# First cross attention: the second temper matmul goes behind the next scores, and the norm's mix and the next group's values change places in the slots

## The chip, the cores and the metric

The kernel runs on one core of a Trainium2 chip (trn2). A core has five engines that run their own instruction queues and meet only through semaphores: PE (TensorE, matmuls and transposes into PSUM), DVE (VectorE), ACT (ScalarE, activation functions), POOL (GpSimd) and SP (here only the issuer of DMAs). The metric is the device time of one execution in microseconds (us), the median over runs.

## The reference

A decoder of two layers works on `x` of 32 sequences x 128 tokens x 128 features and a context of 32 x 77 x 128, all in float32. Each layer is self attention (in the first layer a gated recurrence), cross attention to the context and a feed-forward part, each with a residual and a layer norm. The change is in the first layer's cross attention, which has 16 heads of 8 features:

```python
qk = jnp.einsum('bhqd,bhkd->bhqk', Q, K)
scores = qk / math.sqrt(dk)
mean_sim = scores.mean(axis=(-2, -1))
max_sim = scores.max(axis=-1).mean(axis=-1)
probs = jax.nn.softmax(scores, axis=-1)
entropy_proxy = jnp.var(probs, axis=-1, ddof=1).mean(axis=-1)
feats = jnp.stack([mean_sim, max_sim, entropy_proxy], axis=-1)
hidden = jax.nn.gelu(_linear(feats, w1, b1), approximate=False)
hidden = jax.nn.gelu(_linear(hidden, w2, b2), approximate=False)
log_t = jnp.clip(_linear(hidden, w3, b3), LOG_T_MIN, LOG_T_MAX)
t = jnp.exp(log_t)[..., None]
attn = jax.nn.softmax(qk / (2.0 * t), axis=-1)
out = jnp.einsum('bhqk,bhkd->bhqd', attn, V)
```

So each head of each sequence gets a temperature of its own, from three features of its scores through a small network of three linear steps with two Gelus between them; the real softmax is taken with it. `out` then goes through `Wo`, is added to `x` and normalised.

## The kernel before

`x` stays on chip, transposed, as `xT` (128 features x 4096 tokens). The stages run one after another, each in blocks of its own with its own semaphores. `cross_attention` (line 753) is called twice; only the call with `temper` (the small network's weights) is touched, since the other takes the other list of places.

The 32 sequences stand in 8 groups of 4 (`GB`, `NG`). Work that is done per group: context transpose, keys, queries and values (matmuls over a whole group), the temper network's three matmuls `t1`, `t2`, `t3`, the output projection with the residual (`mix`) and the variance of the norm (`var`). All of these use one PSUM bank, `misc`, in a fixed order: each matmul step waits on `misc_free` until the step before it has been read out, and each reader waits on `misc_mm`. The table `MISC` numbers them in the order in which they stand in `ORDER`.

Work per sequence: `scores` (PE: 8 instructions; DVE: a maximum over the keys, line 1210, then the distance to it, line 1212, each over 128 x 1232), `kbd` (POOL: expands the keys for the scores of the next sequence), `soft` (ACT: exponential, line 1088; POOL: its square), `sums` (DVE: two reductions of them, for the features), `pre` (POOL: distance times the rate), `exp` (ACT, line 1108), `turn` 0 to 3 (PE transposes of the probabilities, evacuated by ACT with Relu, line 1118), `attend` (PE, line 1030), `logs` and `scale` (ACT and DVE: the normalisation of every second sequence's output, line 1248).

There is a software pipeline over slots: slot n works on the scores of sequence n, but on the `pre` and `exp` of sequence n-7, the `turn` of n-8, `attend` of n-9 and the normalisation of n-10. `ORDER` is one list of steps, written out by hand, and every engine goes through the same list and issues its own part of each step; so the list is the queue order of every engine. In each slot it has two places for group work, one after the first two turns and one at the slot's end, after `attend`. `PLACES` says what stands in them in slots 0 to 3 of a group, with an offset of groups: `("values", 1)` are the values of the group after this one, `("mix", -3)` the mix of three groups ago. An entry stands in the list as the step itself (for PE) and then its `_out` (for the engine that reads it from PSUM).

Before, the four slots hold: slot 0 context | keys; slot 1 queries | t1 and t2; slot 2 t3 | values; slot 3 mix | var. The pair `t12` is expanded to `t1, t2, t1_out, t2_out`, so on PE t2 stands right behind t1 and waits on `g1_ready`, which ACT raises in `t1_out`. On ACT, `t1_out` is a Gelu (line 1091) for which a table load is put ahead of it, and `t2_out` (line 1096) is a second Gelu and then an explicit load of the table with Ln and Exp (line 1099):

```python
elif kind == "t2":
    misc(kind, n)
    pe.wait_ge(g1_ready.sem, n + 1)
...
elif kind == "t2_out":
    misc("t2", n)
    f(g2[:, :], ps_m[:, 0:GB * H], ACT.Gelu, bias=mb2[:, :]).then_inc(g2_ready.sem, 1)
    act.wait_ge(g2_ready.sem, n + 1)
    act.sem_inc(misc_free.sem, 1)
    nc.scalar.preload_act_table_set(LN_EXP)
```

`t3` on PE waits on `g2_ready`; `t3_out` on DVE (lines 1239 and 1242) clips; `rate` on ACT (line 1104) makes the factor with which `pre` multiplies. `values_out` is four additions on DVE (line 1198), `mix_out` one on DVE (line 1253, writes `y`), `square` on ACT in slot 3 (line 1128), `var_out` a Ln and an Exp on ACT, and `divide` on DVE in the next slot 0 (line 1258). The step `mean` at the end of slot 2 sums queries and keys on DVE (lines 1230 and 1231).

Of the kernel before, what the change touches and what calls it, by code (L numbers as in the profile page):

```python
# [32 lines left out]
GB = 4  # L33
# [719 lines left out]
def cross_attention(nc, const, tag, xT, context, wq, bq, wk, bk, wv, bv, wo, bo, turn, temper=None):  # L753


    with ExitStack() as ctx:
# [88 lines left out]


        if temper:
            PLACES = [(("context", 1), ("keys", 1)), (("queries", 1), ("t12", -1)), (("t3", -1), ("values", 1)), (("mix", -3), ("var", -3))]
        else:
            PLACES = [(("context", 1), ("keys", 1)), (("queries", 1), ("values", 1)), (None, None), (("mix", -1), ("var", -1))]  # L850

        def place(n, which, read):
            at_ = PLACES[n % GB][which]
            if at_ is None or not 0 <= n // GB + at_[1] < NG:
                return []
            kinds = ("t1", "t2") if at_[0] == "t12" else (at_[0],)
            return [(kind + "_out" * read, n // GB + at_[1], 0) for kind in kinds]

        ORDER = [("bo", 0, 0), ("bo_out", 0, 0)]
        for kind in ("context", "keys", "queries", "values"):  # L860
# [2 lines left out]
        for n in range(B + LA + 4):  # L863
            g, r = n // GB, n % GB
            ORDER += [("scores", n, 0), ("kbd", n + 1, 0)] + [("pre", n - LE, 0)] * bool(temper)
            ORDER += [("turn", n - LT, 0), ("turn", n - LT, 1), ("logs", n - LA - 1, 0), ("scale", n - LA - 1, 0)]
            ORDER += [("divide", g - (4 if temper else 2), 0)] * (r == 0)
            ORDER += place(n, 0, False) + place(n, 0, True)
            ORDER += [("soft", n, 0), ("sums", n - 1, 0)] * bool(temper) + [("exp", n - LE, 0)] * (not temper)
            ORDER += [("turn", n - LT, 2), ("turn", n - LT, 3)]  # L870
            ORDER += [("square", g - (3 if temper else 1), 0)] * (r == 3)
            ORDER += [("exp", n - LE, 0)] * bool(temper) + [("attend", n - LA, 0)]
            ORDER += place(n, 1, False) + place(n, 1, True)
            if temper:
                ORDER += [("feat", g - 1, 0)] * (r == 0) + [("mean", g, 0), ("rate", g - 1, 0)] * (r == 2)
# [1359 lines left out]
def program(nc, a, out):  # L2235

    def of(prefix, *names):
        return [a[f"{prefix}_{n}"] for n in names]

    with ExitStack() as ctx:  # L2240
        xT = ctx.enter_context(nc.sbuf_tensor("xT", [P, NT], F32))
        const = constants(nc, ctx)
        min_gru(nc, const, xT, a["x"], *of("L0_attn", "Wp", "bp", "g1", "Whg", "bhg", "Wo", "bo", "g2", "gf", "Wf", "bf"))
        cross_attention(nc, const, "x0", xT, a["ctx_1024"], *of("L0_xattn", "Wq", "bq", "Wk", "bk", "Wv", "bv", "Wo", "bo"), turn=True,
                        temper=of("L0_xattn", "w1", "b1", "w2", "b2", "w3", "b3"))
        tile_ffn(nc, const, xT, *of("L0_ffn", "signatures_raw", "knot_values", "temperature", "compress_w1", "compress_b1",
                                    "compress_w2", "compress_b2", "spline_w1", "spline_b1", "spline_w2", "spline_b2",
                                    "directions", "norm_gamma", "norm_beta", "output_scale"))
        self_attention(nc, const, xT, *of("L1_attn", "adaptive_scale", "Wq", "bq", "Wk", "bk", "Wv", "bv", "Wo", "bo", "gamma", "beta"))
        cross_attention(nc, const, "x1", xT, a["ctx_1024"], *of("L1_xattn", "W_Q", "b_Q", "W_K", "b_K", "W_V", "b_V", "W_O", "b_O"), turn=False)  # L2250
        moe_ffn(nc, const, xT, *of("L1_ffn", "w_gate", "w_expert", "b_expert"), out)
# [16 lines left out]
```

## Time and profile before

| what | value |
|---|---|
| median of 3 runs | 2020.5 us (2016.04 to 2021.6) |
| profiled execution | 2020.03 us, span 2018.3 us |
| busy over the whole span | PE 84%, PE weight loads 49%, DVE 62%, ACT 59%, POOL 20% |
| mean granted TensorE clock | 0.911 of full |
| first cross attention with its norm | about 737 to 1036 us of the span |

Times are counted from the start of the span. In a timeline each line gives the start, the time (of the merged group where it ends in xN), the engine, the line of the kernel, the operation, what it writes and reads, and in brackets how long the engine had idled before it and what ended that. PEld is the weight load of PE, which overlaps its matmuls. The granted clock is a share of 2.4 GHz; 0.5 is 1.2 GHz.

### The profile page before, as it was taken

The page shows a single profiled execution, that of the slowest core. Times are in us where ns is not written, and L with a number is a line of the kernel's source. Part 1 is how long each engine was busy: PE and PEld are TensorE (multiplying, and loading weights), DVE is VectorE, ACT ScalarE, POOL GpSimd, SP SyncE. Part 2 cuts the span into 40 slices and gives each one's busy share as a digit, 9 for nine tenths or more (in the row PEclk, how much of TensorE's full clock was granted, in tenths as well). Part 3 has the DMA queues.
Part 4 walks back from the last instruction along what each step waited for, and adds up shares of the span by engine and source line. Part 5 has one row for each costly group of instructions (what it writes and reads, how often), then busy time and mean ns, then how long its engine had stood idle before and what let it go on. Part 6 is the DMA issues. An engine that isn't in the chain of part 4 may idle for free. (4 is left out here: it accounts for less than half of the span.)

```text
span 2018.3 us, 30939 instructions
## 1 busy us (share of the span) xinstructions
PE 1695.7 (84%) x11538; PEld 988.3 (49%) x11538; DVE 1252.9 (62%) x1715; ACT 1200.1 (59%) x2551; POOL 400.2 (20%) x369
## 2 busy tenths in 40 slices
PE   3999999999999636888776938999999998688876
PEld 1444444444443213666663414666666666466655
DVE  0777777777778358887527434566666666466644
ACT  2777777787777415787842434555565564355654
POOL 0111011011111026666600001222222222101100
PEclk9999999999999866898975778999999999699997
DMA  4000000000000000000000010000000000000001
GB/s 120 1 11 1 0 7 5 0 0 0 0 0 0 0 21 7 5 5 2 2 4 0 0 42 1 1 1 1 1 1 1 1 1 1 20 8 8 2 4 47
DMA packets 36812, 16.90 MB, mean 8 GB/s; under 512 B 15334, under 2 KB 35520, under 8 KB 36672
## 3 DMA queue, kind: packets, MB, share of 16 engines
q1 hardware_dynamic: 32512, 9.11, 2.0%
q10 hardware_dynamic: 4160, 5.90, 0.9%
q8 instruction: 91, 1.49, 0.3%
q14 instruction: 49, 0.40, 0.1%
HBM read 12.90 MB, written 2.10 MB: 7 GB/s over the span
## 5 line engine op out<-in xcount | busy, mean ns | idle before, releaser
L1967 POOL TENSOR_TENSOR self_probs<-self_probs,self_rz 128x1024 f32<-128x1024 f32 x64 | 121.4, 1897 | 539.5 <-DVE self_rz L1995 539.5
L525 POOL TENSOR_SCALAR gru_decay<-gru_zgate 128x512 f32<-128x512 f32 x96 | 75.8, 790 | 590.7 <-ACT gru_zgate L478 565.5
L1942 ACT ACTIVATE self_probs<-self_scores,self_neg 128x128 f32<-128x128 f32 x512 | 181.9, 386 | 16.6 <-DVE self_neg L1990 16.6
L389 PE MATMUL gru_gate<-gru_xn,gru_whg 128*128 128x512 f32 x384 | 182.4, 597 | 3.5 <-DVE gru_xn L568 3.5
L393 PE MATMUL gru_hid<-gru_xn,gru_whg 128*128 128x512 f32 x384 | 180.4, 592 | 0.0
L401 PE MATMUL gru_out<-gru_y,gru_wo 128*128 128x512 f32 x384 | 178.1, 599 | 0.7 <-DVE gru_y L596 0.6
L1016 PE MATMUL x_turned<-const_ident,x_probs 128*77 128x128 f32 x1024 | 153.0, 297 | 14.2 <-ACT x_pt L1118 9.9
L1118 ACT ACTIVATE x_pt<-x_turned 77x512 f32<-77x512 f32 x224 | 122.1, 584 | 62.9 <-PE x_turned L1016 62.7
L1016 PEld LDWEIGHTS x_turned<-const_ident,x_probs 128*77 128x77 f32 x1024 | 124.6, 159 | 65.2 <-issue 28.7
L1210 DVE TENSOR_REDUCE x_m<-x_scores 128x16 f32<-128x1232 f32 x64 | 91.8, 1434 | 94.8 <-PE x_scores L1005 94.8
L591 DVE SCALAR_TENSOR_TENSOR gru_ghid<-gru_hid,gru_half_c,gru_sighid 128x512 f32<-128x512 f32 x96 | 71.8, 748 | 113.6 <-ACT gru_sighid L479 113.5
L596 DVE TENSOR_TENSOR_SCAN gru_y<-gru_decay,gru_value 128x516 f32<-128x516 f32 x96 | 118.3, 1232 | 3.3
L389 PEld LDWEIGHTS gru_gate<-gru_xn,gru_whg 128*128 128x128 f32 x384 | 72.7, 191 | 94.9 <-issue 94.3
L401 PEld LDWEIGHTS gru_out<-gru_y,gru_wo 128*128 128x128 f32 x384 | 70.2, 190 | 98.4 <-issue 76.1
L393 PEld LDWEIGHTS gru_hid<-gru_xn,gru_whg 128*128 128x128 f32 x384 | 73.1, 190 | 92.3 <-issue 92.3
L1942 ACT ACTIVATION_READ_ACCUMULATOR self_probs<-self_scores,self_neg 128x1 f32 x512 | 115.9, 226 | 0.0
L478 ACT ACTIVATE gru_zgate<-gru_gate,gru_bhg_c 128x512 f32<-128x512 f32 x96 | 66.0, 687 | 67.0 <-PE gru_hid L393 66.3
L344 PE MATMUL gru_stat<-gru_sq,const_ones 128*128 128x512 f32 x144 | 77.2, 626 | 28.6 <-DVE gru_sq L572 28.6
L1928 ACT ACTIVATE self_qT<-self_bank,self_bq,self_scale 128x512 f32<-128x512 f32 x50 | 39.4, 788 | 96.0 <-PE self_bank L1864 96.0
L458 ACT ACTIVATE gru_sq<-gru_h 128x512 f32<-128x512 f32 (+1 forms) x128 | 76.8, 629 | 32.5 <-DVE gru_h L601 30.2
L1030 PE MATMUL x_out<-x_pt,x_vpad 77*32 77x128 f32 x2048 | 69.5, 276 | 30.1 <-DVE x_oT L1248 17.7
L1212 DVE TENSOR_TENSOR x_dist<-x_scores,x_m 128x1232 f32<-128x1232 f32 x64 | 92.2, 1441 | 2.2
(356 smaller groups left out, 3544.5 us busy)
## 6 DMA issues: line engine op xcount, KB each, us to landing
gru_whg<-in_L_attn_Whg ACTq DMA_DIRECT2D x4, 768.0 KB, 10.0
x_ctx_in<-in_ctx SPq DMA_DIRECT2D x16, 154.0 KB
gru_xin<-in_x SPq DMA_DIRECT2D x8, 256.0 KB, 2.9
out<-moe_y SPq DMA_DIRECT2D x8, 256.0 KB, 2.3
gru_wo<-in_L_attn_Wo ACTq DMA_DIRECT2D x4, 384.0 KB, 10.9
self_w_raw<-in_L_attn_Wq SPq DMA_DIRECT2D x1, 512.0 KB, 6.1
self_w_raw<-in_L_attn_Wk ACTq DMA_DIRECT2D x1, 512.0 KB, 6.8
self_w_raw<-in_L_attn_Wv SPq DMA_DIRECT2D x1, 512.0 KB, 9.2
```

The source lines that it names most:

```text
L344: mm(ps_stat[u][:, :], const["ones"][:, :], sq[u][:, 0, :], start=True, stop=True).then_inc(done.sem, 1)
L389: mm(ps_gate[n % 2][:, :], whg[:, l, k, DI + c * P:DI + (c + 1) * P], xn[u][:, k, :], start=(k == 0), stop=(k == KH - 1))
L393: last = mm(ps_hid[n % 2][:, :], whg[:, l, k, c * P:(c + 1) * P], xn[u][:, k, :], start=(k == 0), stop=(k == KH - 1))
L401: last = mm(ps_out[m][:, :], wo[:, l, c, m * P:(m + 1) * P], padded(y[u][:, c, :]), start=(c == 0), stop=(c == KI - 1))
L458: f(sq[u][:, m, :], hidden_chunk(u, i, m), ACT.Square).then_inc(sq_ready[u].sem, 1)
L596: v.tensor_tensor_scan(y[u][:, c, :], decay[r][:, :], value[r][:, :], 0.0, ALU.mult, ALU.add).then_inc(scan_ready.sem, 1)
L1016: last = turn_(ps_t[c % 2][0:S, j * T:(j + 1) * T], probs[n % 2][:, TILE4 * j + c, :], ident[:, :])
L1118: f(pt[n % 2][:, c, :, :].rearrange("p j t -> p (j t)"), ps_t[c % 2][0:S, :], ACT.Relu).then_inc(pt_ready[c].sem, 1)
L1210: v.tensor_reduce(top, scored(), AX.X, ALU.max).then_inc(m_ready.sem, 1)
L1212: v.tensor_tensor(dist[:, n % RING, :, :].rearrange("p (r i) s -> p r i s", i=TILE4), scored(), top.unsqueeze(3).broadcast_to([P, TILE4, T ...
L1942: last = f(probs[n % 2][:, a, jj, :], ps_s[n % 2][:, a, jj * T:(jj + 1) * T], ACT.Exp, bias=neg[n % 2][:, a, jj:jj + 1], accum_out=z[n % 2 ...
L1967: pool.tensor_tensor(probs[n % 2][:, :, :, :], probs[n % 2][:, :, :, :], whole, ALU.mult).then_inc(pn_ready.sem, 1)
```

## The change

The list of places is rewritten and the expansion of an entry changes. After it the four slots hold: slot 0 context | keys; slot 1 queries | t1; slot 2 t2 and t3 | mix; slot 3 values | var. The entry `t23` is expanded to `t2, t2_out, t3, t3_out`, all in its place, so on PE t3 follows t2 directly, and on ACT the second Gelu stands behind the evacuations of turns 0 and 1 of slot 2. `t1_out` stands at the end of slot 1 as before. The offsets in groups stay. No instruction of the kernel's own is added, removed or resized.

```diff
         if temper:
-            PLACES = [(("context", 1), ("keys", 1)), (("queries", 1), ("t12", -1)), (("t3", -1), ("values", 1)), (("mix", -3), ("var", -3))]
+            PLACES = [(("context", 1), ("keys", 1)), (("queries", 1), ("t1", -1)), (("t23", -1), ("mix", -3)), (("values", 1), ("var", -3))]
         else:
...
             at_ = PLACES[n % GB][which]
             if at_ is None or not 0 <= n // GB + at_[1] < NG:
                 return []
-            kinds = ("t1", "t2") if at_[0] == "t12" else (at_[0],)
-            return [(kind + "_out" * read, n // GB + at_[1], 0) for kind in kinds]
+
+            if at_[0] == "t23":
+                return [] if read else [(kind, n // GB + at_[1], 0) for kind in ("t2", "t2_out", "t3", "t3_out")]
+            return [(at_[0] + "_out" * read, n // GB + at_[1], 0)]
```

## Rows read from the trace of the kernel before

**Rows 1.** Windows: busy us of each engine, clock, DMA; steady part of the stage.
```profile
780.00:960.00 180.00, 146.94 (x1942) 110.82 (x1945) 146.53 (x158) 133.05 (x199) 120.29 (x94) 0.86 0.01 4
```

**Rows 2.** Waits of the whole stage: us in total, times, longest us.
```profile
DVE x_m L1210 <- PE x_scores L1005: 37.8, 15, 4.4
...
PE x_misc L1042 <- ACTq L1093: 16.2, 8, 2.8
```

**Rows 3.** Timeline, group 4: end of slot 1 and begin of slot 2.
```profile
868.11 0.39 PE L1037 MATMUL x_misc<-x_var_f,x_w1b 128*128 128x64 f32 x2
868.72 1.28 ACT L1091 ACT_TABLE_LOAD   x1
...
870.02 0.31 ACT L1091 ACTIVATE x_g<-x_misc,x_mb 128x64 f32<-128x64 f32 x1
...
870.48 0.41 PE L1042 MATMUL x_misc<-x_g,x_w2T 128*128 128x64 f32 x2 [1.98 <-ACTq L1093]
...
870.81 0.80 PE L1005 MATMUL x_scores<-x_kbd,x_q 32*128 32x308 f32 x8
870.92 0.32 ACT L1096 ACTIVATE x_g<-x_misc,x_mb 128x64 f32<-128x64 f32 x1 [0.59 <-PE x_misc L1042]
...
871.75 1.44 DVE L1210 TENSOR_REDUCE x_m<-x_scores 128x16 f32<-128x1232 f32 x1 [3.44 <-PE x_scores L1005]
...
872.48 0.33 PE L1046 MATMUL x_misc<-x_g,x_w3b 128*128 128x64 f32 x2
872.63 1.08 ACT L1118 ACTIVATE x_pt<-x_turned 77x512 f32<-77x512 f32 x2
```

**Rows 4.** Timeline, group 4: rest of slot 2 and begin of slot 3.
```profile
873.28 1.15 PE L1016 MATMUL x_turned<-const_ident,x_probs 128*77 128x128 f32 x8 [0.46 <-ACT x_pt L1118]
...
874.77 1.23 ACT L1088 ACTIVATE x_e<-x_dist 128x1232 f32<-128x1232 f32 x1 [1.06 <-DVE x_dist L1212]
...
876.24 1.10 PE L995 MATMUL x_misc<-x_w_v,x_cT 128*77 128x128 f32 x8
...
877.80 0.87 DVE L1198 TENSOR_TENSOR x_vpad<-x_misc,x_bv_row 77x128 f32<-77x128 f32 x4
...
879.07 1.02 PE L1050 MATMUL x_misc<-x_oT,x_w_o 128*128 128x512 f32 x2
...
879.57 1.43 DVE L1210 TENSOR_REDUCE x_m<-x_scores 128x16 f32<-128x1232 f32 x1
```

**Rows 5.** Group 5: its scores and first values in slot 2, and a window there.
```profile
902.47 0.80 PE L1005 MATMUL x_scores<-x_kbd,x_q 32*128 32x308 f32 x8
...
908.82 1.10 PE L995 MATMUL x_misc<-x_w_v,x_cT 128*77 128x128 f32 x8
...
904.00:908.00 4.00, 4.00 (x56) 3.84 (x58) 3.82 (x5) 3.04 (x5) 0.21 (x1) 0.66 0.00 0
```

**Rows 6.** Timeline, group 4: slot 3, `mix_out`, and attention behind DVE's normalisation.
```profile
882.72 0.74 DVE L1253 SCALAR_TENSOR_TENSOR x_y<-x_misc,x_b_o,xT 128x512 f32<-128x512 f32 x1
882.86 1.08 PE L1030 MATMUL x_out<-x_pt,x_vpad 77*32 77x128 f32 x32 [1.89 <-DVE x_oT L1248]
```

**Rows 7.** Timeline, groups 1 and 2: the maximum in slot 2.
```profile
776.51 1.44 DVE L1210 TENSOR_REDUCE x_m<-x_scores 128x16 f32<-128x1232 f32 x1 [2.48 <-PE x_scores L1005]
...
805.84 1.44 DVE L1210 TENSOR_REDUCE x_m<-x_scores 128x16 f32<-128x1232 f32 x1 [4.37 <-PE x_scores L1005]
```

**Rows 8.** Timeline, group 8: the last t2, after the last scores.
```profile
997.40 0.41 PE L1042 MATMUL x_misc<-x_g,x_w2T 128*128 128x64 f32 x2 [1.25 <-ACTq L1093]
```

**Rows 9.** Timeline: the maximum in slot 0 of groups 5 and 6.
```profile
887.39 1.44 DVE L1210 TENSOR_REDUCE x_m<-x_scores 128x16 f32<-128x1232 f32 x1 [1.00 <-PE x_scores L1005]
...
921.40 1.44 DVE L1210 TENSOR_REDUCE x_m<-x_scores 128x16 f32<-128x1232 f32 x1 [2.85 <-PE x_scores L1005]
```

**Rows 10.** Timeline of ACT in the first attention: sigmoid table load and a Square.
```profile
119.16 1.28 ACT L481 ACT_TABLE_LOAD   x1
...
122.01 1.29 ACT L458 ACTIVATE gru_sq<-gru_h 128x512 f32<-128x512 f32 x2 [1.56 <-DVE gru_h L601]
```

## Prediction

> **What bounds the kernel now.** I read the busy shares by slices first, then the windows of the stage that the diff touches, then its waits, and last its timeline step by step. The first cross attention runs from about 737 to 1036 us. In its steady part no engine is full: PE is busy 147 us of 180, DVE 147, ACT 133, POOL 120, and PE's clock averages 0.86 [rows 1]. So the stage is a ring of short waits, and a step is worth what it puts on the ring. Two waits stand out [rows 2]: DVE waits 37.8 us in 15 places for scores, and PE waits 16.2 us in 8 places ahead of the second temper matmul (t2). They are one thing. Rows 3 show it: ACT loads the Gelu table from 868.72 for 1.28 us and writes g1 until 870.33. PE has ended t1 at 868.50 and stands at t2 (start 870.48) with nothing done. The scores queued behind t2 start at 870.81, and DVE, free since 868.31, starts its maximum at 871.75 after 3.44 us of idling.
>
> **Part 1: t2 leaves the end of slot 1.** Nothing is added or removed in number: 8 t1, 8 t2, 8 t3, 8 mixes, 8 values before and after. With t2 behind the next slot's first two turns, the scores follow t1 at once: 868.50 for 870.81, 2.31 us earlier. Their other conditions hold: the distance of the sequence before is long done, and the expanded keys that they read were made a slot earlier by POOL. DVE's maximum then starts at 869.44, and its idling falls from 3.44 to 1.13 us.
>
> **Part 2: what is late next.** t2 must still wait for g1, so it runs at about 870.48 as before, now behind scores and turns. ACT has two evacuations (1.08 us [rows 3]) queued ahead of t2's Gelu: 870.33 + 1.08 = 871.41, and g2 is written at 871.73. t3 stands directly behind t2 on PE and takes g2 at about 871.88 (0.15 after g2, as t2 stands after g1). So the change adds a wait: t3 on PE, t2's end (870.89) to 871.88, 1.0 us. Behind it on PE stand turns 2 and 3, the attention and then the matmul of the slot's last place. Before, t3 started at 872.48 and the values at 876.24, 3.76 us later, of which 0.46 was turn 2 waiting for an evacuation [rows 4]; that wait is covered now. So the mix starts at 871.88 + 3.30 = 875.18, 1.06 us earlier than the values did, and ends at 876.2.
> On DVE the run from the maximum to the bias addition of the values was unbroken, 871.75 to 877.80; moved by 2.31 it ends at 875.49. The mix's addition that takes its place waits there until 876.3, 0.8 us. Queued behind that wait are the two sums over queries and keys and the maximum of sequence 3, which was at 879.57 and comes 1.5 us earlier. The second temper table load now lies between g2 and the softmax exponential: 871.73 + 1.28 = 873.0; the exponential ran at 874.77 before, so it comes 1.8 us earlier and is no bound.
> That is a group at full clock. In the next group turns and t3 ran at half clock (0.66 over 904 to 908), and scores to values took 6.35 us, not 5.43 [rows 5]. With those 0.92 us kept, the mix comes at 902.13 + 4.70 + 0.92 = 907.8 (t2 near 902.13, 0.34 ahead of its scores), its addition at 908.9, where the values ended on PE at 909.9 and none of their additions could start before: 1.0 us gained.
>
> **Part 3: the exchange of mix and values.** Each is about 1.0 us on PE (mix 1.02, values 1.10) and 0.8 us on DVE (0.74 plus issue, 0.87), so slot 2 gets no longer; I count it as zero, between -0.1 and +0.1 a group. In slot 3 the variance matmul waits for the square, which ACT makes behind its evacuations at the same place of the order as before; an earlier y doesn't move it. The attention of slot 3 waits 1.89 us for DVE's normalisation [rows 6], which stands right behind sequence 3's distance. This is why a gain in slot 2 is carried on in full: slot 3 starts from DVE. The values have 0.88 us on DVE between the normalisation and the sums, as the mix's addition had, and POOL's next keys stay behind the sums in the same place. SP's context load isn't passed by any moved step.
>
> **Sum, by group of four sequences** (t2 stands in eight of them). Group 1: nothing turns or mixes yet and DVE is the bound; its 2.48 us [rows 7] go: 2.5. Group 2: no mix yet, half clock; 4.37 us [rows 7] fall to the same 1.1: 3.3, or 2.2 if the softmax behind ACT's second load binds. Groups 3 to 6: 4 x (1.0 to 1.5) = 4 to 6; I take 5.2, since fewer gaps speak for the full clock. Group 7: it had no values in slot 2 and now has a mix there, costing 0.9 of DVE: 0 to 0.7, taken 0.5. Group 8, after the last scores: PE's 1.25 us ahead of t2 [rows 8] are filled by turns, less the wait at t3: 0.6 to 1.0, taken 0.9. Sum 12.4 us, ends 9.3 and 13.7. The profiled execution took 2020.03 us (span 2018.3), 0.5 below the median of 2020.5; so 2020.0 - 12.4 = 2007.6 for its like, and I state 2008 for the median.
>
> **Rivals.**
> *The stall moves instead of going.* In all steady groups the new chain (evacuations, second Gelu, t3, turns, attention, mix) ends as late as the old one. For it: ACT holds that chain, and 1.0 us of PE wait is new. Against it: 1.0 us replaces 2.0. Worth: 2.5 + 2.2 + 0.9 = 5.6, so 2014.4.
> *The clock gains too.* After the t2 gap came half clock in group 5 [rows 5], and another such stretch stood at the seam of slots 3 and 0 of most groups. There DVE idled 2.85 us for scores, but 1.00 where the clock was full [rows 9]; up to 1.85 us each at four seams. A denser slot 2 may spare them: up to 7.4 more, so 2000. Against it: the gap that stands just ahead of those stretches (1.89 us [rows 6]) stays.
> *Slower: the evacuations between the two Gelus force table loads.* They are Relus, and t1's Gelu now leaves its table in place under them. If Relu weren't in that table, a load would go before them and one again before g2. Place: ACT between 870.33 and 871.41. Each is 1.28 us, so g2 is 2.6 us later (874.3), t3 at 874.45, mix at 877.75, its addition at 878.9 for the values' 877.80: 1.1 us lost a group, 8 in all with the softmax behind a third load, so 2028. It decides as soon as more than 16 loads stand in the stage. Against it: in the first attention Squares run right behind a sigmoid table load with no load of their own [rows 10], so simple functions are found in more than one table.
> By the Trainium skill, "ScalarE: Activation LUTs", section on table sets, calls should be batched by set, which speaks against putting other work between two Gelus; but the same section says relu and copy are in every set, which makes no further load. The trace has no Relu under Gelu's table; rows 10 agree for Square. The page also gives a switch as 1.28 us of load plus 1.38 us of drain; the rows show g1 starting 0.02 us after its load ended, so the measured 1.28 stands, and by the page's sum two further switches would cost 5.3 us a group.
> *The exchange doesn't help or the order is bound elsewhere (no change)*: it would need POOL as the bound of slot 2; POOL is busy 120 us of 180 and the least loaded of the four [rows 1]. Small.
>
> **Chances.** Forecast, 2006 to 2011: 0.56. Stall moved, 2012 to 2017: 0.18. Clock gains, 1999 to 2005: 0.15. Slower by reloads, about 2028: 0.05. No change or another loss (half clock added at the one seam that had none, 1.85 us, with stretches longer elsewhere): 0.06. Range 1999 to 2016. A measurement of this kernel can tell about 0.3%, 6 us, from no change. Stall moved lies about that bound and gives half its chance to each side: faster 0.56 + 0.15 + 0.07 = 0.78, same 0.14, slower 0.08.
>
> **What the profile after would show.** PE's wait at line 1042 (after: two lines lower) near zero, a new wait of about 1 us at t3 in front of its Gelu; DVE's total wait for scores down by about 15 us from 37.8; the mix's addition on DVE waiting 0.8 us in slot 2; 16 table loads in the stage, as before; the span of the stage 12 us shorter and the later stages unchanged. The prediction is wrong if the maximum of sequence 3 comes no earlier after that of sequence 0, if the seam stretches at half clock change in number, or if loads are added.

## The result, and the profile after

The changed kernel takes 2001.6 us (median of 4 executions, 1995.8 to 2007.7), the kernel before 2020.9 (median of 4). The ratio is 0.9915, with a 95% interval of 0.9893 to 0.9936: faster by about 17 us, 0.85%. A second measurement, beside the experiments below, gave 1997.5 against 2016.7 and a ratio of 0.9904 (0.9887 to 0.9921). The stated 2008 lies above both medians, by 6.4 and by 10.5 us. The first lies inside the stated range of 1999 to 2016; the second, in a set whose kernel before was 4 us lower too, lies 1.5 us below it. The profiled execution of the first set was its slowest, 2007.7 us with a span of 2006.0.

The page of the changed kernel: busy times are those of before, what went is idle time.

```profile
span 2006.0 us, 30939 instructions
...
PE 1693.5 (84%) x11538; PEld 981.4 (49%) x11538; DVE 1253.5 (62%) x1715; ACT 1198.3 (60%) x2551; POOL 399.5 (20%) x369
```

The waits of the stage in the changed kernel (us in total, times, longest), which answer to [rows 2]:

```profile
DVE x_m L1212 <- PE x_scores L1007: 18.0, 12, 3.2
...
DVE x_y L1255 <- PE x_misc L1052: 15.0, 8, 7.5
...
PE x_misc L1048 <- ACTq L1100: 7.8, 8, 1.0
```

DVE's waiting for scores fell from 37.8 to 18.0 us. PE's wait ahead of t2 (16.2 us before) shrank to 3.3, and t3 got one of 7.8 us in 8 places: the added wait of the prediction. A third stands on DVE, for the mix: 0.51 us in each of groups 3 to 7, and 12.4 us ahead of the three mixes that come after the last scores.

The timeline of group 4 in the changed kernel, the same stretch as [rows 3] and [rows 4] (start us, duration, engine, line, what; idle before it):

```profile
859.01 0.39 PE L1039 MATMUL x_misc<-x_var_f,x_w1b 128*128 128x64 f32 x2
859.33 0.80 PE L1007 MATMUL x_scores<-x_kbd,x_q 32*128 32x308 f32 x8
859.63 1.28 ACT L1093 ACT_TABLE_LOAD   x1
...
860.27 1.44 DVE L1212 TENSOR_REDUCE x_m<-x_scores 128x16 f32<-128x1232 f32 x1 [1.05 <-PE x_scores L1007]
...
860.93 0.31 ACT L1093 ACTIVATE x_g<-x_misc,x_mb 128x64 f32<-128x64 f32 x1
861.39 0.41 PE L1044 MATMUL x_misc<-x_g,x_w2T 128*128 128x64 f32 x2 [0.23 <-ACTq L1095]
861.41 1.08 ACT L1120 ACTIVATE x_pt<-x_turned 77x512 f32<-77x512 f32 x2 [0.17 <-ACT x_g L1093]
...
862.38 0.31 ACT L1098 ACTIVATE x_g<-x_misc,x_mb 128x64 f32<-128x64 f32 x1
862.79 1.28 ACT L1101 ACT_TABLE_LOAD   x1
862.84 0.41 PE L1048 MATMUL x_misc<-x_g,x_w3b 128*128 128x64 f32 x2 [1.05 <-ACTq L1100]
864.09 1.23 ACT L1090 ACTIVATE x_e<-x_dist 128x1232 f32<-128x1232 f32 x1
...
867.11 0.75 DVE L1255 SCALAR_TENSOR_TENSOR x_y<-x_misc,x_b_o,xT 128x512 f32<-128x512 f32 x1 [0.51 <-PE x_misc L1052]
...
868.07 0.69 DVE L1232 TENSOR_REDUCE x_qs<-x_q 128x4 f32<-128x512 f32 x1 [0.21 <-DVEq L1257]
...
869.06 1.43 DVE L1212 TENSOR_REDUCE x_m<-x_scores 128x16 f32<-128x1232 f32 x1
```

The scores now start 0.32 us after the start of t1's last matmuls, where it was 2.70 us. DVE idles 1.05 us before the maximum, not 3.44. The evacuations (Relu, line 1120) run between the two Gelus without a table load of their own: the stage has 8 loads at each of the two lines, as before. t3 waits 1.05 us. The mix's addition waits 0.51 us, and 0.21 us more pass before the next operation on DVE, since `mix_out` waits on its own result before it gives the bank free.

Where the time went, from the starts of DVE's maxima in the two profiled executions. The first number of a pair is before, the second after; seam means sequence 3 of a group to sequence 0 of the next:

```
                        before   after   gained
seq 0 to seq 4           22.73   22.53     0.2
group 1 (seq 4 to 8)     27.44   24.86     2.6
group 2                  31.39   26.87     4.5
groups 3 to 6, seq 0-3   97.75   89.55     8.2
their four seams         36.25   36.70    -0.5
group 7, seq 0-3         23.04   22.42     0.6
seq 31 to last mix       56.26   58.03    -1.8
whole                   294.86  280.96    13.9
```

The step from sequence 1 to sequence 2 shows the gain apart from the clock. Group 4 before and after, as windows (in the order: PE, PEld, DVE, ACT, POOL busy, granted clock, DMA share, GB/s):

```profile
862.44:871.75 9.31, 6.54 (x100) 5.03 (x98) 5.84 (x7) 8.10 (x14) 8.79 (x8) 1.00 0.01 2
853.35:860.27 6.92, 6.14 (x98) 4.73 (x96) 5.84 (x7) 6.41 (x11) 6.39 (x7) 1.00 0.01 2
```

The clock is 1.00 in both, and the step is 2.39 us shorter; groups 5 and 6 give 2.3 and 2.5 at 0.99 to 1.00. The step from sequence 2 to 3 gives part of it back: 0.97 us in group 4 (7.82 to 8.79, full clock in both), 0.45 us in groups 5 and 6, where it ran at a granted 0.80 before and at 1.00 after.

### The profile page after: what moved, and what is told of

It is laid out like the page before. It is cut to its first block and busy times, and to the rows that moved or that the text cites. A ratio compares the mean times of both kernels' runs of the same rounds, so it can differ in the third digit from the quotient of the medians.

```text
span 2006.0 us, 30939 instructions
## 1 busy us (share of the span) xinstructions
PE 1693.5 (84%) x11538; PEld 981.4 (49%) x11538; DVE 1253.5 (62%) x1715; ACT 1198.3 (60%) x2551; POOL 399.5 (20%) x369
## 5 line engine op out<-in xcount | busy, mean ns | idle before, releaser
L1018 PE MATMUL x_turned<-const_ident,x_probs 128*77 128x128 f32 x1024 | 144.8, 286 | 15.5 <-ACT x_pt L1120 8.4
L1018 PEld LDWEIGHTS x_turned<-const_ident,x_probs 128*77 128x77 f32 x1024 | 117.7, 152 | 63.0 <-issue 23.2
```

The source lines that it names most:

```text
L1018: last = turn_(ps_t[c % 2][0:S, j * T:(j + 1) * T], probs[n % 2][:, TILE4 * j + c, :], ident[:, :])
```

## The experiments

The theory tested (A): the scores of slot 2 were held up in PE's queue behind a matmul that waited for ACT, and the exchange of mix and values does nothing. The rivals are these: B, what was gained is TensorE's half clock that goes with the gap; C, the exchange carries part of it; and the reload rival of the prediction.

**The changed kernel again.**

> The changed kernel itself, timed once more beside the others of this set. Theory A (scores were held up in PE's queue by t2): a ratio to the kernel before of 0.991 to 0.994, that is 12 to 18 us. Rival B (most of the gain is the half clock that goes): the gain varies between executions by several us with where the half clock falls.

Measured: 1997.5 us, ratio 0.9904 (0.9887 to 0.9921). The stage (first maximum to last mix addition) took 279.0 us in this trace, 281.0 in the first. Two groups out of the four had the full clock at the seam here, one in the first trace. Theory A had said 0.991 to 0.994; the ratio is a little beyond that, with 0.991 inside its interval. The clock at the seams differs between executions of one kernel.

**t2 moved alone.**

```diff
-PLACES = [(("context", 1), ("keys", 1)), (("queries", 1), ("t1", -1)), (("t23", -1), ("mix", -3)), (("values", 1), ("var", -3))]
+PLACES = [(("context", 1), ("keys", 1)), (("queries", 1), ("t1", -1)), (("t23", -1), ("values", 1)), (("mix", -3), ("var", -3))]
```

> The changed kernel with mix back in slot 3 and the values back in slot 2; only t2 is moved behind the next scores. Theory A: within 2 us of the changed kernel, rather below it, since the tail is spared the mix after slot 38's attention (1.0 us) and group 7 has no mix in slot 2. Rival C (the exchange carries part of the gain): 3 us or more above the changed kernel.

Measured: 1995.4 us, ratio 0.9895 (0.9876 to 0.9913), not slower than the full change; the intervals overlap, the median is 2.2 us lower. The stage took 275.0 us in its trace, 4 to 6 below the two of the changed kernel. C falls.

**The exchange alone.**

```diff
-PLACES = [..., (("queries", 1), ("t12", -1)), (("t3", -1), ("values", 1)), (("mix", -3), ("var", -3))]
+PLACES = [..., (("queries", 1), ("t12", -1)), (("t3", -1), ("mix", -3)), (("values", 1), ("var", -3))]
```

> The kernel before with the exchange of mix and values alone; t2 stays at the end of slot 1. Theory A: within 2 us of the kernel before. Rival C: 4 us or more faster than it.

Measured: 2026.1 us, ratio 1.0040 (1.0027 to 1.0054): slower by 8 us. Theory A had said within 2, so it was wrong on the exchange, too: it has a price. Part of it can be pointed at. After the last scores the groups run on with no DVE work beside them, and the order of PE is the bound. PE of the changed kernel around slot 38, where the mix now stands behind the attention:

```profile
1005.28 1.10 PE L1018 MATMUL x_turned<-const_ident,x_probs 128*77 128x128 f32 x8
...
1008.66 1.06 PE L1032 MATMUL x_out<-x_pt,x_zpad 77*32 77x128 f32 x32
1009.65 1.12 PE L1052 MATMUL x_misc<-x_oT,x_w_o 128*128 128x512 f32 x2
1010.61 1.04 PE L1018 MATMUL x_turned<-const_ident,x_probs 128*77 128x128 f32 x8
...
1013.71 1.08 PE L1032 MATMUL x_out<-x_pt,x_vpad 77*32 77x128 f32 x32 [0.61 <-DVE x_oT L1250]
```

And PE of the kernel before, slots 38 and 39, with the mix between the turns:

```profile
1019.38 1.10 PE L1016 MATMUL x_turned<-const_ident,x_probs 128*77 128x128 f32 x8
...
1023.74 1.10 PE L1016 MATMUL x_turned<-const_ident,x_probs 128*77 128x128 f32 x8
1024.68 1.02 PE L1050 MATMUL x_misc<-x_oT,x_w_o 128*128 128x512 f32 x2
1025.54 1.04 PE L1016 MATMUL x_turned<-const_ident,x_probs 128*77 128x128 f32 x8
1026.90 1.08 PE L1030 MATMUL x_out<-x_pt,x_vpad 77*32 77x128 f32 x32 [0.33 <-DVE x_oT L1248]
```

Slot 38 is 4.36 us long before and 5.33 after, and slot 39 up to its attention 3.16 and 3.10. Between the turns the mix was free, since PE would have waited for ACT's evacuation and DVE there; behind the attention it costs 0.97 us. From sequence 31 to the last mix the kernels with the mix in slot 2 took 58.0, 57.6 and 59.2 us (changed twice, exchange alone), the kernel before 56.3 and 57.2 in its two traces, t2 alone 55.5. In the steady groups sequence 2 to 3 takes 8.53 to 8.58 us with the exchange alone, 8.33 and 7.82 without it; with t2 moved, 8.79 with it and 8.59 without. That is 0.2 us a group, the 0.21 us of `mix_out` waiting on itself. Group 7, which had no values in slot 2, pays more: sequence 0 to 3 takes 24.55 us with the exchange alone and 23.04 before, 22.42 and 20.84 with t2 moved. Group 2 has no mix yet and is 1.8 us shorter; a seam more at half clock costs 1.6. The whole stage took 299.6 us in this trace, 4 to 5 over the two of the kernel before; the other 3 to 4 of the 8 us aren't accounted for.

**t3 moved further, with its reader behind the sums.**

```diff
-                return [] if read else [(kind, n // GB + at_[1], 0) for kind in ("t2", "t2_out", "t3", "t3_out")]
+                return [] if read else [(kind, n // GB + at_[1], 0) for kind in ("t2", "t2_out")]
...
             ORDER += [("turn", n - LT, 2), ("turn", n - LT, 3)]
+            ORDER += [("t3", g - 1, 0), ("t3_out", g - 1, 0)] * bool(temper and r == 2)
```

> The changed kernel with t3 moved once more, from behind t2 to behind turns 2 and 3 of slot 2. Theory A, with the new wait of 1.04 us at t3 being a price: that wait is covered by the turns, the mix comes some 0.6 us earlier in each of six groups, so 2 to 4 us below the changed kernel. If that wait cost nothing (DVE is the bound of slot 2): within 1 us.

Measured: 2008.9 us, ratio 0.9960 (0.9943 to 0.9977), 11 us slower than the changed kernel. The wait at t3 did go, but the trace shows another in its place. DVE, POOL and PE of this kernel:

```profile
866.84 2.24 POOL L1160 TENSOR_TENSOR x_e1sq<-x_e 128x1232 f32<-128x1232 f32 x1 [2.68 <-ACT x_e L1091]
867.17 0.27 DVE L1242 TENSOR_SCALAR x_lt<-x_misc,x_mb 128x64 f32<-128x64 f32 x1
...
867.56 1.12 PE L1053 MATMUL x_misc<-x_oT,x_w_o 128*128 128x512 f32 x2 [0.92 <-DVEq L1244]
867.60 1.53 DVE L1245 TENSOR_SCALAR x_lt<-x_lt 128x64 f32<-128x64 f32 x1
...
869.05 0.74 DVE L1256 SCALAR_TENSOR_TENSOR x_y<-x_misc,x_b_o,xT 128x512 f32<-128x512 f32 x1
```

The second clipping, from SBUF to SBUF, took 1.53 us (median of 8; 0.20 in the other kernels) and ended at 869.13, just behind POOL's square (866.84 + 2.24 = 869.08). It had come into the time in which POOL squares. And the mix waits 0.92 us for the bank, which the first clipping gives free late. Sequence 2 to 3 takes 9.33 us for 8.79 here, at full clock in both. The stage took 285.5 us, 4.5 to 6.5 more than in the two traces of the changed kernel, and none of its four seams was at full clock; the rest of the 11 us isn't accounted for.

**The reload rival's price.**

```diff
                         act.wait_ge(g1_ready.sem, n + 1)
                         act.sem_inc(misc_free.sem, 1)
+                        nc.scalar.preload_act_table_set(LN_EXP)
```

> The changed kernel with a load of the Ln and Exp table right behind the first Gelu, so that two more table loads (1.28 us each) stand between the two Gelus of each group, 32 in the stage and not 16. This is the price of the reload rival. By my sum: about 1.1 us a group slower than the kernel before, so 16 to 24 us above the changed kernel. If ACT had slack there: under 8 us above the changed kernel.

Measured: 2038.4 us, ratio 1.0106 (1.0080 to 1.0133), 37 to 41 us above the changed kernel's medians, more than the 16 to 24 expected. The stage had 32 loads. DVE's waits in it:

```profile
DVE x_y L1256 <- PE x_misc L1052: 30.0, 7, 7.5
DVE x_lt L1242 <- PE x_misc L1048: 28.9, 8, 8.9
```

The clipping waits 28.9 us in total, 6.5 in the changed kernel, and the sums are queued behind it; my sum had moved only PE's chain. PE's wait at t3 grew from 1.05 to 3.69 us in group 4, and half clock followed it (turns at 1.94 us, attention at 1.94). Sequence 2 to 3 took 15.2 us there, not 8.8. So the place is sensitive: 2.57 us more on ACT cost 6.4 us, the half clock included.

**The gap filled in the kernel before.**

```diff
                     elif kind == "t2":
+                        if n:
+                            pe.wait_ge(pt_ready[2].sem, n * GB - 2)
+                        for _ in range(14):
+                            mm(ps_t[0][:, 0:T], ident[:, :], ident[:, :], start=True, stop=True)
```

> The kernel before with 14 matmuls of 128 columns that nobody reads put on PE between t1 and t2, which fill its wait of 2.0 us for the first Gelu. Theory A: no gain, within 2 us of the kernel before, since the scores still stand behind t2. Rival B (the gap brings the half clock, and this costs the time): the stretches at half clock in slot 2 go, and 3 to 6 us are gained.

Measured: 2020.4 us, ratio 1.0011 (0.9998 to 1.0024): no gain. The clock did change. Its windows around slot 2 of groups 3 and 4 (the column ahead of the last two is the granted clock; the kernel before had 0.79 in group 3 over 838 to 846):

```profile
870.00:886.00 16.00, 13.58 (x167) 11.14 (x169) 11.38 (x17) 10.85 (x17) 9.34 (x8) 1.00 0.00 1
840.00:849.00 9.00, 8.47 (x119) 6.38 (x112) 8.25 (x13) 7.25 (x12) 2.62 (x3) 1.00 0.01 3
```

Sequence 2 to 3 took 7.82 us in all four groups, where before it was 8.46, 7.82, 8.33 and 8.34: the half clock costs 0.5 us there. But the filling ran past the wait, and DVE idled 4.40 us for the scores, 0.96 more than before, in each of groups 3 to 7. That price of some 5 us could hide the 3 to 6 us of rival B, so the total alone decides nothing; the step does. The clock in slot 2 of groups 3 to 6 is worth 1.7 us in all, and the step from sequence 1 to 2 gained its 2.4 us a group at full clock in both kernels. As the main cause, B falls.

**The gap of slot 3 filled in the changed kernel,** with 14 and with 8 matmuls:

```diff
+                        if temper and n % GB == 2 and (n + LA) // GB + 1 < NG:
+                            for _ in range(14):
+                                mm(ps_m[96:128, 0:T], ident[:, 0:32], ident[:, :], start=True, stop=True)
                         if n % 2 == 0 and n:
                             pe.wait_ge(o_ready.sem, n // 2)
```

> The changed kernel with 14 matmuls of 128 columns and 32 rows that nobody reads put on PE in slot 3 ahead of the attention that waits 1.8 us for DVE's normalisation. Rival B: the half clock at the seam of slots 3 and 0 goes, and up to 1.5 us is gained in each of four or five groups, 4 to 7 us. If the gap isn't what brings it: within 2 us, or slower by the time that the filling takes beyond the wait.

> The changed kernel with 8 matmuls that nobody reads ahead of slot 3's attention, where 14 ran 1.2 us past the wait. If the gap brings the half clock at the seam of slots 3 and 0: full clock in every group there, sequence 3 to the next sequence 0 takes 7.8 to 8.0 us in each (9.3 to 9.9 at half clock), and 2 to 4 us below the changed kernel. If not: half clock in two or three groups and the changed kernel's time.

Measured: 1999.9 us, ratio 0.9905 (0.9881 to 0.9929) with 14, and 2000.5 us, 0.9919 (0.9897 to 0.9942) with 8: the changed kernel's time. With 14, all four seams took 8.4 us, none 9.3 or more, and the granted clock was 1.00 all through groups 3 to 7; so the gap is what brings the half clock there. The stage took 279.7 us all the same: the attention started 0.8 us later than it had to (not 1.2, as the second expectation has it), which makes the seams 0.5 us longer than at full clock without filling, and the seam after group 2, where PE had waited only 0.48 us, took 8.6 us for 6.6. With 8 the seams took 7.8, 7.8, 8.1 and 7.8 us. But in this trace the half clock stood in slot 2 of group 3. Its windows there:

```profile
829.00:833.00 4.00, 2.49 (x20) 2.09 (x19) 3.44 (x5) 3.72 (x6) 2.81 (x2) 1.00 0.00 2
833.00:837.00 4.00, 4.00 (x67) 3.51 (x66) 2.61 (x2) 3.64 (x6) 2.24 (x1) 0.53 0.01 4
```

Sequence 2 to 3 took 11.6 us there, 9.0 in the changed kernel. The seams gained 3 us over the changed kernel's second trace, this one place cost 2.5. Whether the filling moved the half clock there isn't shown: PE waited the same 0.47 us at t2 and 1.04 us at t3 in that slot of the changed kernel, at full clock, and this is one trace.

**t3 behind the turns, its reader left in place** (on t2 moved alone).

```diff
-                return [] if read else [(kind, n // GB + at_[1], 0) for kind in ("t2", "t2_out", "t3", "t3_out")]
+                return [] if read else [(kind, n // GB + at_[1], 0) for kind in ("t2", "t2_out", "t3_out")]
...
             ORDER += [("turn", n - LT, 2), ("turn", n - LT, 3)]
+            ORDER += [("t3", g - 1, 0)] * bool(temper and r == 2)
```

> The kernel with t2 moved alone (mix and values in their old places), and t3 on PE behind turns 2 and 3 of slot 2, while the clipping on DVE stays ahead of the sums. In the trial with t3 later, the clipping also came behind the sums and its second operation took 1.5 us where it takes 0.2. If PE's wait of 1.04 us at t3 is a price and that long clipping was what made the other trial slower: 0 to 3 us below the kernel with t2 moved alone, and the second clipping at 0.2 us again. If t3's place itself is what costs: slower than it by 5 us or more.

Measured: 2001.6 us, ratio 0.9921 (0.9900 to 0.9943), against 0.9895 (0.9876 to 0.9913) for t2 alone. That is some 5 us slower, where 0 to 3 us faster was expected, and 5 or more was the sign that t3's place itself costs; but the intervals overlap. In the trace, which is of the fastest execution of the five, the clipping took 0.20 us again, and sequence 2 to 3 8.14 us, not 8.59. The stage came out at 275.2 us, as with t2 alone, since a seam more (the one after group 2) was at half clock. So the covered wait at t3 is worth 0.45 us in that step, and no gain in the time; how the 11 us of the trial before divide between the long clipping and t3's place is not settled.

**t1 behind the scores as well, and the clipping between the two sums** (on the kernel just shown; the first sum gets a step `zsum` of its own).

```diff
+            ORDER += [("t1", g - 1, 0), ("t1_out", g - 1, 0)] * bool(temper and r == 2)
-            ORDER += [("soft", n, 0), ("sums", n - 1, 0)] * bool(temper) + ...
+            ORDER += [("soft", n, 0), ("zsum", n - 1, 0)] * bool(temper) + [("t3_out", g - 1, 0)] * bool(temper and r == 2) + [("sums", n - 1, 0)] * bool(temper) + ...
```

> As the one before, with t1 also behind the scores of slot 2 (ACT's table load needs nothing of t1 and covers it) and the clipping on DVE between the two reductions of the sums. If DVE in slot 2 is the bound once PE's queue is free: the maximum of sequence 2 starts with at most 0.3 us of idling where it was 1.05, sequence 3 comes 0.7 us earlier in each of seven groups, 3 to 5 us below the kernel with t2 moved alone. If PE is the bound there: the same time as that kernel.

Measured: 1992.9 us, ratio 0.9878 (0.9852 to 0.9904), the lowest of all and faster than both kernels by its median. Slot 2 of group 4 in it:

```profile
859.31 0.20 DVE L1247 TENSOR_SCALAR x_lt<-x_lt 128x64 f32<-128x64 f32 x1
...
860.44 1.10 PE L999 MATMUL x_misc<-x_w_v,x_cT 128*77 128x128 f32 x8
...
861.57 0.88 DVE L1202 TENSOR_TENSOR x_vpad<-x_misc,x_bv_row 77x128 f32<-77x128 f32 x4 [0.72 <-PE x_misc L999]
```

DVE's idling for the scores is 0.24 us there, but it idles 0.72 for the values: in slot 2 the bound has passed to PE. Sequence 0 to 3 of group 5 takes 21.46 us for 22.22 with t2 alone, and the stage took 271.8 us for 275.0, about what was expected. But the interval overlaps that of t2 alone, and just overlaps those of the changed kernel, so a gain over either isn't clear of the noise.

**The kernel before again.**

> The kernel before once more, for a second trace. Where the half clock falls at the seams of slots 3 and 0 decides 1.5 to 2 us a group; if this is a matter of phase, another group than in the first trace has the full clock. The stage from the first maximum to the last mix took 294.9 us in the first trace; within 4 us of that is expected.

Measured: 2015.9 us, ratio 1.0001 (0.9983 to 1.0018). The stage took 295.8 us, 294.9 in the first trace. In the first trace the full clock stood at the seam after group 4, in this one at the one after group 3 (idle before the maximum of sequence 16):

```profile
852.78 1.44 DVE L1210 TENSOR_REDUCE x_m<-x_scores 128x16 f32<-128x1232 f32 x1 [1.00 <-PE x_scores L1005]
```

## Why the prediction was right, and where it was off

**The mechanism held.** The scores follow t1 at once (predicted 2.31 us earlier, measured 2.38); DVE's idling of 1.13 us is 1.05; the new wait at t3 of 1.0 us is 1.05; the second table load is no bound; the mix's addition waits, 0.51 us where 0.8 was predicted, plus 0.21 for its own result. In group 4, at full clock in the first trace of each kernel, sequence 0 to 3 takes 22.42 us for 23.83: 1.41 gained, 1.5 predicted. Group 1 gained 2.6 (2.5), group 7 0.6 (0.5).

**The term for groups 3 to 6 was mis-sized,** 5.2 predicted, 8.2 measured within the groups. I gave a group 1.0 us with the half clock kept in slot 2 and 1.5 without any, and had no case in which it goes. In both traces of the kernel before three of these four groups had it (granted clock 0.80 or 0.81), in both of the changed kernel none has (1.00), and the gains are 1.9 us (group 5) and 2.0 (group 6). Group 3 gained 2.9, of which 1.2 in the step from sequence 0 to 1, at a granted 0.76 before and 1.00 after. Group 2, 3.3 predicted, gained 4.5: t2 alone gives 3.7 there, and the exchange 0.8, since the group has no mix yet and the values leave its slot 2.

**The clock at the seams** was the second rival, and most of its 7.4 us didn't come. One of four seams was at full clock in both first traces, another one each; in the second traces it was one before and two after. By my own sign, a change in that number, the second pair speaks against the forecast and the first doesn't. With t2 in its old place four traces have one, one, none and none at full clock (before twice, exchange alone, its gap in slot 2 filled), with t2 behind the scores six have one, two, two, two, two and none (the last is the trial with t3 and its reader late). So a small part of rival two, 1.5 us a seam, may be in the gain; these are too few traces to tell it from chance.

**The wrong step is part 3,** that the exchange counts as zero. For the steady groups it was 0.2 us, twice my bound. For the tail I hadn't asked what covers the mix: group 8 was to gain 0.9, and from sequence 31 on 1.8 us were lost in the first traces, 0.4 in the second. With t2 moved alone 0.8 to 1.8 us were gained there, so it is the exchange that turned this term around. The exchange alone made the kernel before 8 us slower. So the gain comes from the move of t2, and the exchange takes some of it back: 2 us by the medians, 4 to 6 by the traces of the stage.

**The reload rival** didn't happen: 8 loads stand at each line, with Relus between the Gelus. By the Trainium skill, "ScalarE: Activation LUTs", section on table sets, relu is in every set; the trace agrees. Its price was under-sized, at 8 us over the kernel before where the trial measured 20, because the clipping on DVE and the sums behind it hang on t3 too.

**Where the sum was helped by luck.** The stage got 13.9 us shorter in the first traces, against a sum of 12.4, because the errors have opposite signs: 4.2 us too little for groups 2 to 6, 2.7 too much for the tail and 0.5 lost at the seams. The high end of the sum is also added up wrong, 13.5 and not 13.7 us; and half of the chance of a stall that moves is 0.09, not the 0.07 that was added to faster.

**What stays open.** The traces of the stage show 14 to 17 us of gain, the two measurements 17 to 19. Outside the stage the code is the same, and yet the part up to the first maximum varies between 736.5 and 741.1 us and the part from the last mix on between 976 and 986 over the traces. A few us of the difference may be this, or chance; no run tells.

## What to carry to other kernels

In a queue that is one list for all engines, a matmul that waits for another engine costs what stands behind it, not its own time: put it behind work whose inputs are there, and look at what then stands in front of its successor. When two steps of the same size change places, ask for each place what covers it, in the tail as well as in the steady part; a place between two steps that wait for an evacuation is free, one at a slot's end isn't. Undo each half of a double change alone: here one half brought all of the gain and the other took some back.

## What the runs showed of the hardware

- A DVE operation of 128 x 64 elements from SBUF to SBUF took 1.53 us in place of 0.20 when it fell into POOL's tensor_tensor of 2.24 us, and ended 0.05 us after it; in seven of eight groups of that run it overlapped POOL's square, took 0.73 to 1.79 us and ended 0.05 or 0.06 us after it, and in the eighth, with nothing on POOL, it took 0.20. The one ahead of it, which reads PSUM, took its usual 0.27, and reductions took their 1.43 us beside POOL too. The Trainium skill, "SBUF — State Buffer", section "SBUF: two separate sides", says that DVE in a 2-port mode and POOL hold a shared port pair as an exclusive lock for a whole instruction; the trace agrees in its times, and doesn't show the mode.
- TensorE's half clock (1.2 GHz) came behind PE's waits of 1.98 us at t2 and of 1.60 to 1.78 us ahead of slot 3's attention, but not behind each: in group 4 of the kernel before the clock stayed full after 1.98 and after 1.89 us, and two seams of the changed kernel's second trace stayed full after 1.77 to 1.78 us. Filling a wait with matmuls kept the clock full there: in slot 2 of all groups in the kernel before, at the four seams in the changed one. In slot 2 the half clock cost 0.5 us of DVE's time a group, at the seam 1.5.
- A table load costs ACT 1.28 us and nothing that the trace shows beside it: the exponential behind the load at 862.79 starts at 864.09 in the changed kernel.
